# Modulation of a norm applied per channel behind the transpose, and its inverse root on Pool, in a four-layer transformer kernel

## What is computed

```python
mod = silu(c) @ w_adaln + b_adaln                     # six vectors of 144 for each sequence
sh_msa, sc_msa, g_msa, sh_mlp, sc_mlp, g_mlp = split(mod, 6)
h = ln(x) * (1 + sc_msa) + sh_msa
o = softmax(q @ k.T * 9 ** -0.5) @ v                   # q, k, v from h @ w_qkv + b_qkv
x = x + g_msa * (o @ w_proj + b_proj)
h = ln(x) * (1 + sc_mlp) + sh_mlp
x = x + g_mlp * mlp(h)     # layer 0: the two best of four experts, weighted; layer 1 and 2: one MLP
```

## Time and profile before

| | us |
|---|---|
| median of three runs | 918.87 (909.43 to 920.58) |
| the profiled execution | 919.2 |
| its span on the core | 917.2 |
| PE busy | 751.5 (82%) |
| DVE busy | 556.0 (61%) |
| ACT busy | 386.0 (42%) |
| POOL busy | 181.0 (20%) |

### The profile page before, as it was taken

How to read it: one execution, slowest core, us unless ns; L and a number is a source line. 1 busy time by engine, 2 the same in 40 slices (tenths; PEclk the granted TensorE clock), 3 DMA queues, 4 the chain that set the end, 5 groups by cost and what they waited for, 6 DMA issues and landing times.

```text
span 917.2 us, 11092 instructions
## 1 busy us (share of the span) xinstructions
PE 751.5 (82%) x3571; PEld 438.5 (48%) x3571; DVE 556.0 (61%) x1614; ACT 386.0 (42%) x690; POOL 181.0 (20%) x372
## 2 busy tenths in 40 slices
PE   6597889967998799798867886979897789979746
PEld 1353444335764445366444343645443555436325
DVE  3477787886327558752465777474787666785242
ACT  0221465534444544254235442435453356646511
POOL 5502012440132300302323003021003110021020
PEclk9955899989997669799977997976897988999957
DMA  3210100110121000012100000100000101000000
GB/s 88 69 35 7 32 14 22 39 31 13 48 56 32 1 24 13 12 33 60 39 18 1 24 12 13 32 1 1 24 13 11 33 1 25 12 12 1 13 1 13
DMA packets 22714, 21.23 MB, mean 23 GB/s; under 512 B 4831, under 2 KB 17015, under 8 KB 22658
## 3 DMA queue, kind: packets, MB, share of 16 engines
q1 hardware_dynamic: 22610, 20.52, 8.6%
q10 hardware_dynamic: 48, 0.02, 0.0%
HBM read 13.62 MB, written 0.61 MB: 16 GB/s over the span
## 4 chain that ended last, share of the span: by engine, by line
PE 62%; DVE 28%; issue 4%; ACT 2%; POOL 2%; DMA 0%; DVEq 0%; SPq 0%; ACTq 0%; POOLq 0%
PE m_bank L1400 11%; PE o_bank L1422 10%; DVE row_max L972 9%; PE s_bank L1383 8%; PE d_bank L1539 7%; PE d_bank L1483 3%; PE m_bank L1592 3%; PE m_bank L1409 2%; DVE h_tok L1031 2%; PE d_bank L1528 2%; PE d_bank L1440 2%; PE d_bank L1439 1%; PE d_bank L1454 1%; PE d_bank L1530 1%; PE d_bank L1529 1%
## 5 line engine op out<-in xcount | busy, mean ns | idle before, releaser
L797 ACT ACTIVATE probs<-s_bank 128x512 f32<-128x512 f32 x384 | 223.1, 598 | 380.4 <-PE s_bank L1383 377.1
L972 DVE TENSOR_REDUCE row_max<-m_bank 128x1 fp32r<-128x512 f32 x384 | 255.3, 686 | 91.8 <-PE m_bank L1400 86.5
L1400 PE MATMUL m_bank<-k_pad,q_t 128*128 128x512 f32 x348 | 173.1, 511 | 43.0 <-DVE row_max L972 12.6
L1383 PE MATMUL s_bank<-q_t,k_pad 128*128 128x512 f32 x384 | 176.3, 466 | 2.9 <-ACT probs L797 2.0
L1400 PEld LDWEIGHTS m_bank<-k_pad,q_t 128*128 128x128 f32 x348 | 72.1, 212 | 115.0 <-issue 36.8
L1422 PE MATMUL o_bank<-probs,v_aug 128*32 128x512 f32 x768 | 120.6, 704 | 0.7 <-ACT probs L797 0.7
L1383 PEld LDWEIGHTS s_bank<-q_t,k_pad 128*128 128x128 f32 x384 | 81.8, 215 | 30.1 <-ACT probs L797 15.4
L1539 PE MATMUL d_bank<-w,g_act 128*128 128x144 f32 (+1 forms) x480 | 61.8, 288 | 8.7 <-issue 8.7
L1539 PEld LDWEIGHTS d_bank<-w,g_act 128*128 128x128 f32 (+1 forms) x480 | 59.5, 190 | 14.2 <-issue 8.3
L714 POOL TENSOR_TENSOR h_tok<-h_tok,mod 128x144 f32<-128x144 f32 x48 | 23.7, 494 | 202.7 <-DVE h_tok L1031 202.7
L1592 PE MATMUL m_bank<-gram_rows,ident 64*64 64x208 f32 (+42 forms) x128 | 40.3, 403 | 16.0 <-DVE gram_rows L1207 15.6
(11 more groups left out here) (232 smaller groups left out, 1145.1 us busy)
## 6 DMA issues: line engine op xcount, KB each, us to landing
k_pad<-k_t SPq DMA_DIRECT2D x96, 64.0 KB, 2.0
raw_a<-in_L_cond_w_dram SPq DMA_DIRECT2D x10, 288.0 KB
w<-in_L_cond_w_dram SPq DMA_DIRECT2D x10, 288.0 KB
w_rows<-in_L_cond_W_dram SPq DMA_DIRECT2D x8, 141.8 KB
raw_d<-in_L_cond_w_dram SPq DMA_DIRECT2D x30, 36.0 KB
x_tok<-in_x_dram SPq DMA_DIRECT2D x2, 288.0 KB, 4.5
w<-in_L_cond_W_fc_dram SPq DMA_DIRECT2D x2, 288.0 KB
raw_a<-in_L_cond_W_fc_dram SPq DMA_DIRECT2D x2, 288.0 KB
```

Of the source, the lines that this page charges most:

```text
L797: act.activation(probs[:, n % PROBS, :], s_banks[n % S_BANKS][:, :], ACT.Exp, scale=HD ** -0.5)\
L972: dve.tensor_reduce(row_max[:, grp % 2, t, MAXROW + 32 * j:MAXROW + 32 * j + 1], bk[:, :], AX.X, ALU.max).then_inc(drained, 1)
L1383: pe.matmul(s_banks[n % S_BANKS][:, :], k_pad[:, grp % PADS, j, kt * P:(kt + 1) * P], q_t[:, par, g, :], start=True, stop=True).then_inc(s ...
L1400: ins = pe.matmul(bk[:, :], q_t[:, par, g, t * P:(t + 1) * P], k_pad[:, grp % PADS, j, :], start=True, stop=True)
```

## The change

1. `mods(l)` now makes only the shifts and scales, and makes them per channel: the weights are the stationary operand and two columns of silu(c) the moving one. The last 16 channels are made three times, at rows 0, 32 and 64. DVE takes them out by four small operations.
2. The two gates of a layer, which are still needed in every partition, are made by a stage of their own, `gates(l)`, with 288 columns; that of layer 0 is woven in as block 0's first stage instead of standing in HEAD. The DMA of the next layer's weights waits for it.
3. The normalised tiles are transposed without modulation. Behind the transpose ACT applies scale and shift as it rounds (Identity with a scale and a bias per partition), DVE computes the unrounded value of the 128 channels (`h_full`) and subtracts for `h_lo`, and for rows 32 to 64 DVE computes `h_part`, ACT's `h_d` waits for that, and POOL subtracts.
4. The inverse root of "msa" and "mlp" is fourteen dependent operations on POOL. DVE signals it after aggregating (`aggregated`), takes what maxima are left of the step (`fill_all`), and waits for it (`rooted`); the first slot of the norm is still one slot.
5. `x_tok` and `o_tok` have the padded row of `h_tok`, so that "o" and "x" are transposed from where they lie; POOL only copies the 16 channels.

```diff
-        out += [("norm", 1, "msa"), ("qkv", 1), ("prep", 1), ("prep", 2), ("mods", 1, 0), ("prep", 3)]
+        out += [("gates", 0), ("norm", 1, "msa"), ("qkv", 1), ("prep", 1), ("prep", 2), ("mods", 1), ("prep", 3)]
...
-        out += [("mods", 1, 1)]
     if block == 2:
-        out += [("mods", 2, 0), ("prep", LAYER_ITEM[2])]
+        out += [("gates", 1), ("prep", LAYER_ITEM[2])]
     if block == 3:
-        out += [("mods", 2, 1)]
+        out += [("mods", 2)]
     if 1 <= block < BLOCKS - 1:
         out += [("norm", block + 1, "msa"), ("qkv", block + 1)]
+    if block == BLOCKS - 2:
+        out += [("gates", 2)]
...
-HEAD = [("mods", 0, 0), ("mods", 0, 1), ("prep", 0), ("norm", 0, "msa"), ("qkv", 0)]
+HEAD = [("mods", 0), ("prep", 0), ("norm", 0, "msa"), ("qkv", 0)]
...
-    todo += [(LAST_SLOT[("mods", 1, 1)], ("ada", 2))]
+    todo += [(LAST_SLOT[("gates", l - 1)], ("ada", l)) for l in range(1, LAYERS)]
...
-        x_tok = sb("x_tok", [P, B * T, C])
-        mod = sb("mod", [P, B, 2, 6, C])
+        x_tok = sb("x_tok", [P, B, T, P + DW])
+        gates_by = sb("gates_by", [P, B, 2, 2, C])
...
-            link(pool.memset(h_tok[:, :, :], 0.0))
-            for at in (C, P + 64 + CR):
-                link(pool.memset(h_tok[:, :, at:at + 1], 1.0))
+            for tiles in (h_tok[:, :, :], x_tok[:, :, :, :].rearrange("p b t c -> p (b t) c"),
+                          o_tok[:, :, :, :].rearrange("p b t c -> p (b t) c")):
+                link(pool.memset(tiles[:, :, C:], 0.0))
+                for at in (C, P + 64 + CR):
+                    link(pool.memset(tiles[:, :, at:at + 1], 1.0))
...
+                if kind in ("msa", "mlp"):
+                    n = seen.next("rooted")
+                    pool.wait_ge(s["aggregated"], T * n)
+                    y, v, r = rstd[:, :], var_eps[:, :], nwt[:, 0, :]
+                    link(pool.tensor_scalar(v, mean_var[:, :, 1], EPS, None, ALU.add))
+                    link(pool.tensor_scalar(y.bitcast(I32), v.bitcast(I32), -0.5, 1597463007.0, ALU.mult, ALU.add))
+                    for i in range(3):
+                        link(pool.tensor_tensor(r, v, y, ALU.mult))
+                        link(pool.tensor_tensor(r, r, y, ALU.mult))
+                        link(pool.tensor_scalar(r, r, -0.5, 1.5, ALU.mult, ALU.add))
+                        ins = pool.tensor_tensor(y, y, r, ALU.mult)
+                        if i < 2:
+                            link(ins)
+                    ins.then_inc(s["rooted"], 1)
+                    pool.wait_ge(s["rooted"], n)
+                for t in range(T):
+                    if kind == "x":
+                        pool.wait_ge(s["x_done"], blk % B * 2 + t // 2 + 1)
+                    elif kind != "o":
+                        pool.wait_ge(s["xn_ready"], seen.next("xn_ready"))
+                    tile = token_tile(blk, kind, t)
+                    pool.tensor_copy(tile[:, P + 32:P + DW].rearrange("p (r w) -> p r w", r=2)[:, :, 0:CR],
+                                     tile[:, P:C].unsqueeze(1).to_broadcast([P, 2, CR]))\
+                        .then_inc(s["h_tok_ready"], 1)
+                    pool.wait_ge(s["h_tok_ready"], seen.next("h_tok_ready"))
+                yield
+                _, (_, d_free, before) = ring.take(), ring.take()
+                yield
                 seen.next("norm")
-                for t in range(T):
-                    if kind != "o":
-                        pool.wait_ge(s["xn_ready"], seen.next("xn_ready"))
-                    tile = h_tok[:, t, 0:C]
-                    d2 = h_tok[:, t, P + 32:P + DW].rearrange("p (r w) -> p r w", r=2)[:, :, 0:CR]
-                    src = h_tok[:, t, P:C]
-                    if kind in ("msa", "mlp"):
-                        link(pool.tensor_tensor(tile, tile, mv[:, first + 1, :], ALU.mult))
-                        link(pool.tensor_tensor(tile, tile, mv[:, first, :], ALU.add))
-                    elif kind == "o":
-                        link(pool.tensor_copy(tile, o_tok[:, blk % 2, t, :]))
-                    pool.tensor_copy(d2, src.unsqueeze(1).to_broadcast([P, 2, CR]))\
-                        .then_inc(s["h_tok_ready"], 1)
-                yield
-                ring.take(), ring.take()
-                yield
+                if kind in ("msa", "mlp"):
+                    pool.wait_ge(s["h_part_ready"], seen.next("modulated"))
+                    pool.wait_ge(s["h_d_ready"], seen.n["norm"])
+                    pool.tensor_tensor(h_d[32:64, :], h_part[32:64, :], h_d[32:64, :].bitcast(F32), ALU.subtract)\
+                        .then_inc(d_free, 1)
+                    pool.wait_ge(d_free, before + 1)
                 yield
...
+                act.wait_ge(*mods_done[l])
+                act.wait_ge(s["mods_ready"], 3 * (l + 1))
+                shift, scale = mod_a[:, l % 2, v, b:b + 1], mod_a[:, l % 2, v + 1, b:b + 1]
+                act.activation(h_hi[:, :], a_bank[:, :], ACT.Identity, scale=scale, bias=shift)\
+                    .then_inc(s["h_hi_ready"], 1)
+                act.wait_ge(s["h_part_ready"], seen.next("modulated"))
+                act.activation(h_d[:, :], d_bank[0:DW, :], ACT.Identity, scale=mod_d[:, l % 2, v + 1, b:b + 1],
+                               bias=mod_d[:, l % 2, v, b:b + 1]).then_inc(s["h_d_ready"], 1)
...
-                        for i in range(T):
-                            dve.bn_aggr(mean_var[:, i, :], stat[:, i, :]).then_inc(s["dve_done"], 1)
-                        done[0] += T
-                        dve.wait_ge(s["dve_done"], done[0])
-                        link(dve.tensor_scalar(nwt[:, 1, 0:T], mean_var[:, :, 1], EPS, None, ALU.add))
-                        rsqrt(rstd[:, :], nwt[:, 1, 0:T], nwt[:, 0, 0:T])
+                    for i in range(T):
+                        dve.bn_aggr(mean_var[:, i, :], stat[:, i, :]).then_inc(s["aggregated"], 1)
+                    fill_all[0]()
+                    n = seen.next("rooted")
+                    dve.wait_ge(s["aggregated"], T * n)
+                    dve.wait_ge(s["rooted"], n)
                     for t in range(T):
-                        tile = x_tok[:, b * T + t, :]
-                        if kind == "x":
-                            ins = dve.tensor_copy(h_tok[:, t, 0:C], tile)
-                        else:
-                            ins = dve.tensor_scalar(h_tok[:, t, 0:C], tile, mean_var[:, t, 0:1], rstd[:, t:t + 1],
-                                                    ALU.subtract, ALU.mult)
-                        ins.then_inc(s["xn_ready"], 1)
+                        dve.tensor_scalar(h_tok[:, t, 0:C], x_tok[:, b, t, 0:C], mean_var[:, t, 0:1], rstd[:, t:t + 1],
+                                          ALU.subtract, ALU.mult).then_inc(s["xn_ready"], 1)
...
-                dve.wait_ge(s["h_hi_ready"], 2 * seen.n["norm"] - 1)
-                dve.tensor_tensor(h_lo[:, :], a_bank[:, :], h_hi[:, :].bitcast(F32), ALU.subtract)\
-                    .then_inc(a_free, 1)
-                dve.wait_ge(s["h_hi_ready"], 2 * seen.n["norm"])
-                dve.tensor_tensor(h_d[32:64, :], d_bank[32:64, :], h_d[32:64, :].bitcast(F32), ALU.subtract)\
-                    .then_inc(d_free, 1)
+                if kind in ("o", "x"):
+                    dve.wait_ge(s["h_hi_ready"], seen.n["norm"])
+                    dve.tensor_tensor(h_lo[:, :], a_bank[:, :], h_hi[:, :].bitcast(F32), ALU.subtract)\
+                        .then_inc(a_free, 1)
+                    dve.wait_ge(s["h_d_ready"], seen.n["norm"])
+                    dve.tensor_tensor(h_d[32:64, :], d_bank[32:64, :], h_d[32:64, :].bitcast(F32), ALU.subtract)\
+                        .then_inc(d_free, 1)
+                else:
+                    dve.wait_ge(s["h_turned"], T * seen.n["norm"])
+                    dve.tensor_scalar(h_part[32:64, :], d_bank[32:64, :], mod_d[32:64, l % 2, v + 1, b:b + 1],
+                                      mod_d[32:64, l % 2, v, b:b + 1], ALU.mult, ALU.add)\
+                        .then_inc(s["h_part_ready"], 1)
+                    dve.wait_ge(s["h_hi_ready"], seen.n["norm"])
+                    link(dve.tensor_scalar(h_full[:, :], a_bank[:, :], mod_a[:, l % 2, v + 1, b:b + 1],
+                                           mod_a[:, l % 2, v, b:b + 1], ALU.mult, ALU.add))
+                    dve.tensor_tensor(h_lo[:, :], h_full[:, :], h_hi[:, :].bitcast(F32), ALU.subtract)\
+                        .then_inc(a_free, 1)
...
+                for i, v in enumerate((0, 1, 3, 4)):
+                    for ada, c, first in ((ada_a, c_wide_a, True), (ada_d, c_wide_d, False)):
+                        pe.matmul(bk[:, B * i:B * (i + 1)], ada[:, v * C:v * C + P], c[:, :, 0], start=first,
+                                  stop=not first)
+                    for ada, c, first in ((ada_a, c_wide_a, True), (ada_d, c_wide_d, False)):
+                        for r in range(0, DW, 32):
```

(14 more changed lines are left out.)

162 lines of the change are left out of this document (105 added, 57 removed).

## The result

The changed kernel takes 953.17 us, median of four runs (951.41 to 957.37); the kernel before ran 914.15 beside them. The ratio is 1.0382, interval 1.0327 to 1.0436: slower by 35 us. Every ratio here is formed over the undisturbed executions of both kernels and so is not the quotient of the two medians. The forecast was 936.0, 17 us more, with a range of 910 to 952 and "same" as the likeliest class (0.46, against 0.44 for slower). So direction and first cause were right, the size was half of what came, and the measured time lies 1.2 us above the range. A ratio is uncertain by 4 to 10 us, a difference of two ratios by up to 13.

What follows compares the result with a forecast made beforehand. PE and DVE in turn were taken to bound the kernel. Terms +17.6 + 0.8 + 7.2 - 5 + 3 - 1.4 - 3.4 - 1.5 = +17.3 on 919.2, less 0.3, gave 936.2, say 936.0 us; range 910 to 952.

Steps and rivals of the forecast that it cites:

- A: Root on POOL: DVE waits 3.85 us against 2.2 in each of eleven norms, +17.6 us (8.8 to 34).
- B: At 454 us POOL is still rounding the next stage's weights, so the root starts late: +0.8 us.
- C: Third slot, taking out turned tiles: longer DVE path, 1.2 us at six PE waits in the loop, +7.2 (4 to 20).
- D: HEAD: cheaper modulation matmuls bring the first q, k, v product to 30.8 from 35.53 us, -5 (-8.5 to -1).
- G: TAIL: less POOL work in the last norm and fewer copies, less the longer third-slot path: -3.4 us.
- H: Loop: 96 POOL tensor_tensor of 0.49 go, which could hold DVE, and tiles turn sooner: -1.5 us (0 to -3).
- some 60 us: Sign to look for: PE's ten waits behind the first slot, 44.7 us before, grow to this in all.
- R4: Rival, the clock: a stretch at 0.50 comes or goes, about 8 us, 928 to 944; chance 0.05.
- R2: Rival: POOL and DVE block each other in every third slot, +2.0 in ten, 949 us; chance 0.15.
- It decides if `h_lo` is over 1.5 us: Third-slot sign: DVE's h_lo above that length would decide for the rival of POOL and DVE blocking each other.
- E: Block 0: layer 0's gates, four matmuls of 288 columns, now run there: +3 us (1 to 4.9).
- F: Modulation and gates of layers 1 and 2: 6.7 us each after 7.4 before, -1.4 for both (-6 to +4).

Runs made afterwards that it cites:

- root_dve: The changed kernel with the inverse root back on DVE, all else as changed; 934.29 us, ratio 1.0189.
- before_root_pool: The kernel before with only the inverse root moved to POOL; 935.53 us, ratio 1.0203.
- plain_slot: root_dve with the kernel before's third slot for every norm, scale and shift left out, for measuring only; 902.01 us, ratio 0.9826.
- plain_plus_full: plain_slot with one DVE operation added, computing h_full unused ahead of h_lo in the twelve real norms; 915.46 us, ratio 0.9957.
- act_first: root_dve with DVE's h_part waiting for ACT's h_d instead of the reverse, same operations; 942.52 us, ratio 1.0225.
- hd_dve: The changed kernel with the norm's last subtraction (32 x 512) on DVE instead of POOL; 950.75 us, ratio 1.0369.
- gates_head: The changed kernel with gates(0) back ahead of the loop, in HEAD behind mods; 953.27 us, ratio 1.0394.
- both_dve: The changed kernel with both the root and the norm's last subtraction on DVE; 938.15 us, ratio 1.0238.
- scale_first: The kernel before with DVE subtracting mean and multiplying by scale, POOL making and applying the root and adding shift; 912.50 us, ratio 0.9926.

## Why the prediction was right or wrong

| part | forecast, us | measured, us | from |
|---|---|---|---|
| root (A, B) | +18.4 | +17.7; +18.7 | changed against root_dve; before_root_pool against before |
| third slot (C, with its 1.3 in D and 1.2 in G) | +9.7 | +33 | root_dve against plain_slot |
| everything else (D to H without these) | -10.8 | -16 | plain_slot against before |
| sum | +17.3 | +35 | |

**A and B, the root: right in place and in who waits; right in sum by luck.** The order showed DVE with nothing to do, and it stood idle. The step of one operation was put at 0.26 and is 0.28, the gap at 3.85 and is 4.11. Two errors cancelled: DVE's gaps grew by 24 us and not by 18.4, and only three quarters of that reached the end. The sum of PE's ten waits, "some 60 us", came as 60.3, also with help: the wait at 294 us gave 5.1 of the 15.6, most of it for want of the modulation matmuls and not by the root. At 454 the root begins behind POOL's weights, as foreseen, 0.1 after them; DVE idles 7.98 there, where the prediction's times give 6.6.

**C, the third slot: the term that failed, by a factor of three.** The failing step is "behind a third slot PE waits for DVE six times: 6 x 1.2". Its count and its size were wrong, and something stood beside it that C had at nothing.

- The count: all ten places in the loop are hit, the four with a stall under 1 us before too (3.01 us at 599, ended by POOL's subtraction, is the largest of them).
- The size: at the six places of the earlier trace rows the stall grew by 0.9 to 2.2, 1.55 in the mean, over the 1.2 taken. The ten together are 27 us, the six were 11.5, so that the loop has some 15 us where 7.2 were forecast; the stalls ahead of and behind the loop grew by 1.45 each, against 1.3 and 1.2.
- Beside it: these stalls explain the 18.7 us that PE stands longer in root_dve than in plain_slot. The other half of the third slot's price, 16 us, is that PE's own matmuls took longer, at the lower clock. The prediction had that as R4, as a stretch that comes or goes, with a chance of 0.05, and not as something that follows from C.

About 10 to 12 us of the whole belong to `h_full`, as plain_plus_full shows. The other 21 to 23 belong to `h_part` with ACT's wait, and to the fourth operation, whichever engine has it; act_first and hd_dve show that neither ACT's wait nor POOL's place is a price that can simply be taken off, and how this rest is divided among them stays open.

The rule of the Trainium skill weighed there, that a GpSimd instruction reading SBUF and a VectorE one with two SBUF inputs exclude each other ("SBUF — State Buffer", "Who interferes with whom"), is borne out in both directions: POOL's subtraction takes 1.70 beside `h_lo` and 1.26 alone, then holds DVE's L1285 for 0.8. The estimate of 1.25 for POOL's subtraction was right for it alone. Rival R2, "+2.0 in ten, 949", had 0.15 of the chances and was the nearest to what came. "It decides if `h_lo` is over 1.5 us" did not hold: `h_lo` stayed at 0.69, DVE came first by 0.1 us, and the held one was the solver's operation behind it, which the prediction had not looked at.

**D, HEAD: right in sum, with errors that cancel.** First product forecast at 30.8, seen at 30.40. Inside, `mods` took 5.8 us in place of 8.0, since the passes with 32 weight columns cost next to nothing; the start was 1.1 later, and the gap for the root 0.9 longer because POOL was rounding weights until 18.26, while aggregate had ended at 17.52. The prediction looked only for what ran past 18.8. Its dear bound of -1 does not follow from its own prices: 48 passes at 0.11 and the dear root together give about +2.

**E, gates in block 0:** put at 3 (1 to 4.9); gates_head leaves it between 1 and 4. **F:** `mods` takes 4.8 and 3.8 in layers 1 and 2 (forecast 4.2). **G and H** weren't run apart; together with D to F they gave 5 us more than forecast. One part of this the traces show: DVE's four tiles take 1.15 in root_dve and 1.64 in before_root_pool. The single operations say why: the first two last 0.35 us in both, the third and fourth 0.35 in root_dve but 0.54 and 0.65 in before_root_pool, where POOL's multiplications of 128 x 144 run beside them. So it is POOL and not the wider rows of `x_tok`, which would lengthen or shorten all four; over twelve norms it is 6 us of DVE's time.

**The clock (R4): half of the third slot's price.** Four kernels have the same 3739 matmuls on PE:

| | span, us | PE busy | PE standing |
|---|---|---|---|
| plain_slot | 894.3 | 738.6 | 155.7 |
| plain_plus_full | 914.9 | 749.6 | 165.3 |
| root_dve | 929.0 | 754.6 | 174.4 |
| changed | 949.7 | 753.4 | 196.3 |

From plain_slot to root_dve the span grows by 34.7 us; 18.7 of it are standing and 16.0 are the same matmuls being busy longer. From root_dve to the changed kernel all of it is standing. The granted clock fits this: (1 - clock) / 0.5 of the span was at 1.2 GHz, which is 254 us in plain_slot (0.858), 288 in root_dve (0.845) and 304 in the changed kernel (0.84). If one counts busy time in stretches of 0.50 by half, in windows of 1 us, all four kernels come to 635 us, within 1: the same work, more of it at the lower clock. These are single executions.

One place shows it row by row, the third slot of the same norm, first root_dve and then plain_slot:

```profile
582.71 0.77 PE L1615 MATMUL d_bank<-h_hi,ff_hi 128*128 128x512 f32 x1 [3.31 <-POOL h_d L742]
583.27 0.63 PE L1616 MATMUL d_bank<-h_lo,ff_hi 128*128 128x512 f32 x1
583.70 0.63 PE L1617 MATMUL d_bank<-h_hi,ff_lo 128*128 128x512 f32 x1
```
```profile
567.32 0.48 PE L1615 MATMUL d_bank<-h_hi,ff_hi 128*128 128x512 f32 x1 [1.10 <-DVE h_d L1098]
567.63 0.39 PE L1616 MATMUL d_bank<-h_lo,ff_hi 128*128 128x512 f32 x1
567.86 0.39 PE L1617 MATMUL d_bank<-h_hi,ff_lo 128*128 128x512 f32 x1
```

Behind the stall of 3.31 us the matmuls follow each other every 0.43 us for 3.4 us; behind the one of 1.10 the same ones every 0.23. Such a stretch of 3.4 us stands behind three more third-slot stalls of root_dve (3.53 at 104 us, 3.37 at 715, 2.28 at 746), and behind none of their counterparts in plain_slot (1.74 or less). So a longer stall cost there twice, once standing and once behind it. That the clock followed from the stall everywhere is not shown.

The mean granted clock of a whole execution is a poor guide. both_dve has 0.865, as if it had run faster than all of these, but between 39 and 91 us its row grants 1.00 where root_dve has 0.51, and the same 113 matmuls took the same time (PE busy is the number behind "52.00,"; root_dve, then both_dve):

```profile
39.00:91.00 52.00, 45.18 (x113) 22.01 (x113) 35.02 (x110) 10.62 (x22) 2.77 (x9) 0.51 0.11 28
```
```profile
39.00:91.00 52.00, 45.46 (x113) 22.63 (x113) 34.88 (x109) 10.76 (x21) 2.72 (x8) 1.00 0.11 28
```

## What to carry over

Where two engines wait for each other in turn, ask of each added operation not only whether its neighbour waits there now, but whether it stands between two things that both sides need next: here 0.84 us of DVE was paid at about its full length in all twelve norms, while the six stalls that the profile showed made up only half of the places. Where two kernels have the same matmuls, split their difference into PE's standing and PE's busy time: it showed that half of the third slot's price lay in matmuls at the lower clock and not in the stalls, and the mean granted clock did not. Moving a chain of small dependent operations to an idle engine pays only if the first engine has other work to do meanwhile; if it must wait, find what it can do without the result, as scale_first does (0.7% faster than the kernel before). And where an instruction waits for another engine's turn at a shared bank, read both queues: what stands ahead of the one and behind the other is the price.

## What was not expected of the hardware

- A subtraction of 32 x 512 on POOL takes 1.26 alone and 1.70 when it starts 0.1 us after a DVE operation of 0.69 with two SBUF inputs; each held the other in turn. A second POOL operation directly behind did not lengthen the hold: DVE's small one got in between (ended at 222.43, POOL's second began at 222.50).
- DVE's operations on 128 x 144 with one SBUF input, pipelined one behind the other, took 1.15 for four in root_dve and 1.64 in before_root_pool. A single one lasts 0.35 without POOL's multiplication beside it and 0.54 to 0.65 with it.
- Matmul passes of two columns in `HEAD`: two with 128 weight columns take 0.5 us, six with 32 weight columns 0.2, so 0.25 and 0.035 each.
- The granted clock can stand at 1.00 in a record while the matmuls run at the lower speed: 45.46 us for 113 matmuls in both_dve at 1.00, 45.18 for the same in root_dve at 0.51.
